# A mixture-of-experts stage whose hidden features are dealt to the chunks by threes, and whose down weights arrive in longer pieces

## The reference: what is computed

```python
def step(y, params):
    W1e, b1e, W2e, b2e, ge = params
    h = jax.nn.gelu(jnp.einsum('bld,df->blf', x, W1e) + b1e, approximate=False)
    out = jnp.einsum('blf,fd->bld', h, W2e) + b2e
    return (y + ge[..., None] * out, None)
y, _ = jax.lax.scan(step, y0, (W1, b1, W2, b2, gate_e))
```

## Time and profile before

| | |
|---|---|
| median of 3 runs | 806.53 us (803.93 to 810.06) |
| the profiled execution | 807.92 us |
| its span in the profile | 806.1 us |
| PE busy | 704.1 us (87%) |
| L482, up: PE busy, matmuls | 176.8 us, 2844 |
| L494, down: PE busy, matmuls | 174.3 us, 1896 |
| hardware_dynamic transfers | 87.46 MB in 90002 packets |

### The profile page before, as it was taken

One profiled execution on the slowest core, in us unless ns is written; L12 is line 12 of the kernel. 1 busy time (PEld: TensorE's weight loads), 2 busy tenths in 40 slices (PEclk: granted clock), 3 DMA queues, 4 the chain that ended last, 5 costly groups with the idle time before them and its releaser, 6 DMA issues.

```text
span 806.1 us, 22693 instructions
## 1 busy us (share of the span) xinstructions
PE 704.1 (87%) x7841; PEld 599.0 (74%) x7841; DVE 458.6 (57%) x1331; ACT 373.2 (46%) x891; POOL 350.4 (43%) x535
## 2 busy tenths in 40 slices
PE   0775789999999999999798999999999999988980
PEld 0563556777777777776568999998999999988970
DVE  7201446788888888888746663343343444433448
ACT  0232156666666666666363433343343443333353
POOL 7771122567777777777455641222122122211220
PEclk9995579999999999999789999999999999999995
DMA  7726524444444444444048534647347435388258
GB/s 202 134 40 187 130 73 107 103 104 120 109 113 109 113 110 111 110 110 117 16 135 240 145 94 116 183 128 213 103 112 204 112 89 144 107 247 232 83 181 324
DMA packets 98811, 108.98 MB, mean 135 GB/s; under 512 B 16545, under 2 KB 89250, under 8 KB 98402
## 3 DMA queue, kind: packets, MB, share of 16 engines
q1 hardware_dynamic: 90002, 87.46, 41.9%
q0 software_dynamic: 8720, 20.36, 8.5%
HBM read 140.32 MB, written 32.34 MB: 214 GB/s over the span
## 4 chain that ended last, share of the span: by engine, by line
PE 60%; POOL 13%; DVE 11%; issue 11%; ACT 2%; DMA 2%; SPq 1%; POOLq 1%; DVEq 0%; ACTq 0%
PE BK L482 20%; PE BK L494 20%; POOL pixels L1778 4%; PE BK L811 4%; PE BK L937 3%; PE BK L896 3%; PE BK L948 2%; PE BK L916 2%; DVE negmax L1517 2%; POOL slot_rows L1846 2%; POOL rs L1795 2%; DVE hr L687 1%; POOL hr L1835 1%; PE BK L468 1%; PE BK L976 1%
## 5 line engine op out<-in xcount | busy, mean ns | idle before, releaser
L513 ACT ACTIVATE pixels<-BK,b1t 128x128 f32<-128x128 f32 x474 | 131.1, 375 | 217.6 <-PE BK L482 217.6
L697 POOL DMA_INDIRECT pair_rows<-pixels x79 | 75.9, 961 | 249.6 <-DVE pixels L663 243.9
L482 PE MATMUL BK<-pixels,shared 64*128 64x128 f32 x2844 | 176.8, 275 | 6.1 <-issue 5.9
L494 PE MATMUL BK<-shared,pixels 64*128 64x192 f32 x1896 | 174.3, 328 | 6.8 <-issue 4.9
L482 PEld LDWEIGHTS BK<-pixels,shared 64*128 64x128 f32 x2844 | 171.6, 189 | 10.1 <-issue 9.9
L494 PEld LDWEIGHTS BK<-shared,pixels 64*128 64x128 f32 x1896 | 154.7, 187 | 9.8 <-issue 9.6
L1517 DVE TENSOR_REDUCE negmax<-BK 128x6 f32<-128x1536 f32 x64 | 112.4, 1756 | 26.7 <-PE BK L916 25.5
L1278 ACT ACTIVATE shared<-BK 128x1536 f32<-128x1536 f32 x64 | 92.7, 1449 | 9.8 <-PE BK L937 9.3
L1846 POOL DMA_INDIRECT slot_rows<-xr,adr x64 | 64.7, 1010 | 36.6 <-issue 13.8
L661 DVE TENSOR_TENSOR pixels<-BK,shared 128x192 f32<-128x192 f32 x79 | 28.2, 357 | 77.9 <-PE BK L494 77.6
L647 DVE TENSOR_TENSOR pixels<-pixels 128x1 int32<-128x1 f32 x64 | 10.2, 159 | 98.1 <-PE BK L468 98.1
(11 more groups left out here) (240 smaller groups left out, 1040.5 us busy)
## 6 DMA issues: line engine op xcount, KB each, us to landing
shared<-ew SPq DMA_DIRECT2D x158, 288.0 KB
shared<-ew SPq DMA_DIRECT2D x79, 576.0 KB
shared<-qk_parts SPq DMA_DIRECT2D x112, 96.0 KB
pixels<-slot_rows SPq DMA_DIRECT2D x79, 104.0 KB
shared<-eb SPq DMA_DIRECT2D x79, 96.0 KB
qk_parts<-shared SPq DMA_DIRECT2D x32, 192.0 KB, 2.0
shared<-qk_parts SPq DMA_DIRECT2D x16, 288.0 KB
shared<-pair_rows SPq DMA_DIRECT2D x12, 384.0 KB, 7.6
```

The costliest lines, as they stand in the source:

```text
L482: last = nc.tensor.matmul(hidden(t)[h * HC + c], w1h[w][rows, (k + h) % NK, c * P:(c + 1) * P], xtT[p][rows, k, :], start=(c == 0 and k == ...
L494: last = nc.tensor.matmul(Y[h], hT[p][rows, c * P:(c + 1) * P], w2b[w][rows, c, :], start=(c == 0), stop=(c == FC - 1))
L513: last = nc.scalar.activation(hT[p][:, c * P:(c + 1) * P], hidden(t)[c], ACT.Gelu, bias=b1t[:, c, t:t + 1])
L697: nc.gpsimd.indirect_dma_start(pair_d, bass.IndirectOffsetOnAxis(t_dst[:, t:t + 1], 0), ysum[t % NB][:, :], None).then_inc(s[f"m_sc{t % NB ...
```

## The change

Three edits, all of the same renaming of features. Within each half of 384 features, chunk c took features c*128 to c*128+127. Now chunk c takes every third: c, c+3, c+6, ... up to c+381.

- In `w1h`, which lies in SBUF as before, the fixed operand of L482 is then every third column: a step of 3 elements, 12 bytes, where it was 1 element.
- In `b1r`, the bias matmuls (L442, L458) read every third column in the same way.
- In `w2b`, partition p holds for each half the three rows 3p, 3p+1 and 3p+2, which lie side by side in HBM. The transfer is written as 128 partitions x 2 pieces of 576 numbers (2304 bytes) where it was 128 x 6 pieces of 192 (768 bytes). The bytes are the same, 576 KB.

The number of instructions, their order on each engine and their waits are the same. The diff, whole but for its surroundings:

```diff
             def second(t, e, new):
                 w = t % NW
                 wait_prev(sp, s["m_s2"], t - NW + 1)
-                sp.dma_start(w2b[w][:, :, :], ew2[ds(e, 1), :, :].rearrange("a (c p) d -> p (a c) d", p=P),
+                sp.dma_start(w2b[w][:, :, :].rearrange("p (h c) d -> p h (c d)", h=2),
+                             ew2[ds(e, 1), :, :].rearrange("a (h p c) d -> p (a h) (c d)", h=2, p=P),
                              cond=new) \
                     .then_inc(s[f"m_wb{w}"], 16)
...
             for c in range(FC):
-                last = nc.tensor.matmul(M0[:, c * NEARLY:(c + 1) * NEARLY], b1r[:, c * P:(c + 1) * P], b1e[:, 0:NEARLY],
+                last = nc.tensor.matmul(M0[:, c * NEARLY:(c + 1) * NEARLY], b1r[:, c // HC * (FF // 2) + c % HC:(c // HC + 1) * (FF // 2):HC], b1e[:, 0:NEARLY],
                                         start=True, stop=True)
...
             for c in range(FC):
-                last = nc.tensor.matmul(M0[:, c * NREST:(c + 1) * NREST], b1r[:, c * P:(c + 1) * P], b1e[:, NEARLY:NTILE],
+                last = nc.tensor.matmul(M0[:, c * NREST:(c + 1) * NREST], b1r[:, c // HC * (FF // 2) + c % HC:(c // HC + 1) * (FF // 2):HC], b1e[:, NEARLY:NTILE],
                                         start=True, stop=True)
...
                     for h, rows in enumerate((LO, HI)):
-                        last = nc.tensor.matmul(hidden(t)[h * HC + c], w1h[w][rows, (k + h) % NK, c * P:(c + 1) * P],
+                        last = nc.tensor.matmul(hidden(t)[h * HC + c], w1h[w][rows, (k + h) % NK, c:FF // 2:HC],
                                                 xtT[p][rows, k, :], start=(c == 0 and k == 0), stop=(k == NK - 1),
                                                 skip_group_check=True)
```

## The result

The changed kernel takes 876.61 us in the median (871.72 to 879.21, 4 runs), against 808.29 us for the kernel before beside it (803.93 to 810.45, 4 runs): 1.084 times as long, interval 1.080 to 1.089, or 68 us more. The profiled execution has 871.72 us and a span of 869.9. The forecast of 802.5 us was wrong, by sign and by size. What came is rival A in kind; it had put the rise at 56 us, 12 less than the 68 that came.

A forecast was written before the change was run, and what follows sets the result against it. TensorE was taken to bound the expert stage, with some waits for late weights; W2 pieces -4.0 us, issue, bias matmuls and stepped operand nothing, so 806.53 - 4.0 = 802.5 us, range 796 to 878 for 8 in 10.

The forecast's parts named there:

- rival A: Stepped weight load of the up matmuls slows by half: up 2.01 to 2.89 us, net +56 us, about 863 us; chance 0.22.
- What bounds the stage: Expert stage: TensorE bounds it, plus 16.1 us of waits in 25 places, taken as late weight transfers.
- The fixed operand: Up matmuls' weight loads (L482), every third column: cost taken as 0, with ends 0 and 147 us.
- 8 ns of room in a pair: Up matmuls: a half's load fills 104 of a pair's 112 ns; each further 1% of slower load costs 1.6 us.
- The covered waits: Expert stage with slower ups: a slower tile covers most weight waits, so the 16 us come back in part.
- point of decision: Up matmuls' stepped load: the sign turns once the load is over 8% slower, passing +1% at about 16%.
- The W2 pieces: W2 transfers in 2304-byte pieces: 3.4 us from late loads and 0.6 from early ones, -4.0 us in sum.
- the gain of a W2 transfer: Each real W2 load: 1.44 us of full DMA at 410 GB/s instead of 1.65 at 358, 0.21 us less.
- Rival E: W2 pieces change nothing if HBM and W1's two half-width transfers set the full share: 806 us; 0.53 together with the forecast.
- The packets: DMA packets with longer W2 pieces: fewer than 90,002 by some 31 x 512 = 16,000.
- Rival D: Shorter W2 transfers let each following W1 start earlier, lateness does not build up: 10 to 16 us go, 791 to 796; chance 0.07.
- The chances: Whole kernel, about 1% as threshold: faster 0.08, within 1% 0.55, slower 0.37; the forecast with no W2 effect has 0.53.

The follow-up runs named there:

- whole_rows: Kernel before with W1 and W2 laid out in HBM as one 4608-byte piece per partition each, W1 in one 128-partition transfer, step 1: 788.41 us against 809.07, ratio 0.976.
- step 2: Kernel before with the up matmuls' fixed operand taking every second column (only the time counts): 839.35 us, one run, against 840.05.
- w1_one_short: Kernel before with W1 laid out anew in HBM, in one transfer over 128 partitions, three pieces of 1536 bytes a partition: 787.74 us, ratio 0.976.
- w1_two_wide: Kernel before with W1 laid out anew in HBM, in two transfers each over 128 partitions, pieces of 1536 bytes: 822.17 us against 840.91, ratio 0.979.

## Why the prediction was wrong, point by point

**What bounds the stage: right.** TensorE, with waits for weights in runs of real loads. The waits were transfers, as inferred from SyncE's rows and the full DMA share: the completions of W1 and W2 stand 0.09 us ahead of each late up and down, and whole_rows took away all 14.9 us of them.

**The fixed operand: the step that failed.** It cost 1.07 us a tile, 84.5 us over 79. The prediction priced it at 0, "since the rows lie nearer to spare room than to none: the transposes prove a fetch at 0.38 where 0.81 is used". The transposes' loads prove that rate for columns side by side, four to a 16-byte block. Their 128 columns need 32 blocks; the stepped ones need 96. What is scarce is blocks, and no row of the kernel before counted those. (At 0.38 ns a column the transposes spend 1.5 ns a block, so that the 1.8 is the price in this kernel's pairs and not of every load.) The other half of the reading was right and should have weighed more: 8 ns of room in a pair. With so little, whatever the step cost beyond 8% had to show on 2844 instructions of the path.

**Rival A: right in kind, mis-sized in one term.** The pair was put at 161 ns and took 171, the up at 2.89 and took 3.08, so 70 us were forecast for 84.5. The mechanism given for it, one more pass at 0.38 ns a column, was not it. The covered waits, "in part", were 14 in its sum and 14.9 in the profile. Its point of decision, loads 8% slower, is not tested: at step 2 the ups were 5% slower, 9 us in all, but the one run took 839 us where the kernel before scatters from 835 to 847.

**The W2 pieces: mis-sized.** -4.0 us forecast, -0.9 measured (-2.3 to +0.5). The main term that failed is the gain of a W2 transfer: 0.21 us, with the rate taken as 410 GB/s from 3072-byte pieces that read back results at the end of the kernel, where the packets of the stage show 0.08. With that, 16 x 0.21 = 3.4 becomes 1.3. And what made the weights late was W1's transfer, which the change left alone. Rival E named that cause, "W1's two half-width transfers", and w1_one_short and w1_two_wide show it. The packets fell by 14,336, which is 28 x 512: 28 real loads of W2, not 31.

**Rival D: wrong for this change, right on what was there.** The waits could be cured (14.9 us, and 21 of the time), but by W1's width.

**The chances.** 0.37 was on slower, and the range of 796 to 878 reaches just over the 876.6. But the 0.53 of the forecast rested on one unseen cost taken as nothing, where 8 ns of room stood in the rows against it.

## What to carry to other kernels

A matmul's fixed operand in fp32 may be stepped by two columns at little cost (5% of the up here), not by three or more, unless the streaming beside it is long enough to cover about 1.8 ns for each 16-byte block touched. Put a permutation of features into the layout in HBM, not into the access pattern of an instruction that runs thousands of times. Before making pieces longer, see which transfers complete just before the late work begins, and whether those that share the DMA engines with them go to all 128 partitions.

## What the runs showed of the hardware that was not expected

- The load's cost has an edge between steps 2 and 3: 118, then 171, 230 and 235 ns a pair at 2, 3, 4 and 8.
- Transfers to 64 partitions at a time are slow as a pair: in the runs of loads 242 to 287 GB/s. The same W1 in the same 1536-byte pieces over 128 partitions takes away 21 us of 809, and its mean packet goes from 92 to 80 ns.
- A lateness that left TensorE idle for 2.35 us cost nearly as much again, 1.9 us: the granted clock fell to 0.50, and the next 24 matmuls took 3.90 us instead of 2.01.
- A wait that the profile put down to ScalarE was one for W2: the completion of the transfer stood 0.09 us ahead of the start, as at every other wait for weights.
- The kernel before takes 809 us on some chips and 840 on others, so that times compare on one chip only.
